# Four sums moved from POOL to DVE, and SP's flag check put ahead of its waits for the stores

## The reference

```
layer 0: graph attention: softmax over neighbours of leaky(s1_i + s2_j), times h W0
layer 1: attention by relation: scores h_i . (a_r * h_j) for adj == r, leaky, softmax, times h
layer 2: sum over relations r of (adj == r) @ h @ W_r, plus a bias
layer 3: graph attention as layer 0, with W3; its output goes through elu:
         x = x + elu(attention @ (h W3))
```

## Time and profile before

| | |
|---|---|
| three runs, median | 287.89 us |
| the profiled execution | 288.05 us, of which the span is 285.8 |
| PE busy | 274.3 us (96%) |
| ACT, DVE | 255.0 (89%), 251.9 (88%) |
| POOL | 234.1 (82%) |
| granted TensorE clock | 0.997 |

### The profile page before, as it was taken

One profiled execution on the slowest core, in us unless ns is written; L12 is line 12 of the kernel. 1 busy time (PEld: TensorE's weight loads), 2 busy tenths in 40 slices (PEclk: granted clock), 3 DMA queues, 4 the chain that ended last, 5 costly groups with the idle time before them and its releaser, 6 DMA issues.

```text
span 285.8 us, 8113 instructions
## 1 busy us (share of the span) xinstructions
PE 274.3 (96%) x2252; PEld 257.9 (90%) x2252; DVE 251.9 (88%) x1217; ACT 255.0 (89%) x850; POOL 234.1 (82%) x376
## 2 busy tenths in 40 slices
PE   3999999999999999999999999999999999998991
PEld 2999998888889999999999999888889999998991
DVE  4889999988878887899999999998898888799985
ACT  5998988799998888999999999799999889796994
POOL 4998787777747999999999988887755899999722
PEclk9999999999999999999999999999999999999998
DMA  6946645400000000015333201000000000001213
GB/s 216 319 127 179 177 142 147 167 2 2 0 0 3 0 2 2 3 37 150 98 109 114 73 22 41 18 18 2 1 2 1 3 0 0 3 3 54 76 58 115
DMA packets 15414, 17.79 MB, mean 62 GB/s; under 512 B 2180, under 2 KB 11272, under 8 KB 15368
## 3 DMA queue, kind: packets, MB, share of 16 engines
q1 hardware_dynamic: 15220, 17.18, 19.9%
q10 hardware_dynamic: 148, 0.07, 0.1%
HBM read 13.05 MB, written 4.19 MB: 60 GB/s over the span
## 4 chain that ended last, share of the span: by engine, by line
PE 87%; DVE 8%; ACT 2%; issue 1%; POOL 0%; DVEq 0%; POOLq 0%
PE bank L1001 26%; PE bank L943 10%; PE bank L919 9%; PE bank L948 9%; PE bank L877 7%; PE bank L986 5%; PE bank L956 5%; PE bank L968 5%; PE bank L998 4%; PE bank L903 3%; PE bank L950 2%; DVE pT L699 2%; DVE expy L735 1%; PE bank L922 1%; DVE st L624 1%
## 5 line engine op out<-in xcount | busy, mean ns | idle before, releaser
L367 POOL TENSOR_TENSOR rs<-mv,minus_half 128x2 f32<-128x2 f32 x128 | 89.8, 702 | 35.5 <-DVE mv L635 35.0
L1001 PE MATMUL bank<-val,pT 128*128 128x129 f32 x512 | 74.6, 275 | 0.0
L1001 PEld LDWEIGHTS bank<-val,pT 128*128 128x128 f32 x512 | 67.3, 192 | 0.0
L384 POOL TENSOR_TENSOR h<-h,rs 128x256 f32<-128x256 f32 x93 | 58.2, 626 | 2.3
L699 DVE SCALAR_TENSOR_TENSOR pT<-bank,val,edgesT 128x256 f32<-128x256 f32 x128 | 55.0, 471 | 0.8 <-PE bank L956 0.7
L624 DVE BATCH_NORM_STATS2 st<-x 128x6 f32<-128x128 f32 x192 | 45.2, 276 | 0.0
L527 ACT ACTIVATE val<-bank,val 128x128 f32<-128x128 f32 x128 | 44.3, 437 | 0.1
L635 DVE BATCH_NORM_AGGREGATE mv<-st 128x2 f32<-128x9 f32 x256 | 33.5, 172 | 10.8 <-DVE st L624 1.0
L919 PE MATMUL bank<-w_gat,hT 128*128 128x131 f32 x256 | 40.3, 281 | 0.0
L376 POOL TENSOR_TENSOR h<-x,mv 128x256 f32<-128x256 f32 x64 | 40.1, 626 | 0.0
L877 PE MATMUL bank<-ident,h 128*128 128x128 f32 x192 | 38.0, 280 | 1.4 <-ACT hT L495 1.1
(11 more groups left out here) (87 smaller groups left out, 662.7 us busy)
## 6 DMA issues: line engine op xcount, KB each, us to landing
edges<-in_adj SPq DMA_DIRECT2D x32, 256.0 KB, 2.9
xin<-in_x SPq DMA_DIRECT2D x32, 128.0 KB, 2.6
out_x<-result SPq DMA_DIRECT2D x32, 128.0 KB, 1.7
w_rel<-in_L_gnn_weight SPq DMA_DIRECT2D x1, 256.0 KB, 2.8
w_gat<-in_L_gnn_W ACTq DMA_DIRECT2D x1, 64.0 KB
w_gat<-in_L_gnn_W SPq DMA_DIRECT2D x1, 64.0 KB
a_rel<-in_L_gnn_a SPq DMA_DIRECT2D x4, 0.5 KB, 3.0
bias<-in_L_gnn_bias SPq DMA_DIRECT2D x1, 64.0 KB, 3.3
```

What stands on the lines that cost most here:

```text
L367: pool.tensor_tensor(rs[:, n % WIDE], mv[:, n % WIDE, :, 1], minus_half[:, :], ALU.pow).then_inc(rs_ready, 1)
L384: pool.tensor_tensor(h[:, n % HS, :, 0:D], h[:, n % HS, :, 0:D], rs[:, n % WIDE, :].rearrange("p (t o) -> p t o", o=1).to_broadcast([P, T, ...
L1001: last = pe.matmul(bank_o(n)[:, t], pT[:, n % 4, u, t * P:(t + 1) * P], values[:, u], start=(u == 0 and layer == 1), stop=(u == T - 1), sk ...
```

## The change

POOL_SUMS lists the graphs whose sum is made by POOL: every second one among the first sixteen, every fourth among the second sixteen (16, 20, 24, 28). DVE_SUMS are the others. `summed(g)` gives the semaphore (0 for POOL, 1 for DVE) and the count that say that the sum of g is there; the waits of SP, ACT and DVE use it. On SP, the waits for the stores go behind the load of the flag and the branch, and into the general path's start.

```diff
+POOL_SUMS = [g for g in range(B) if g % (2 if g < 16 else 4) == 0]
+DVE_SUMS = [g for g in range(B) if g not in POOL_SUMS]
...
+def summed(g):
+
+    return (0, POOL_SUMS.index(g) + 1) if g in POOL_SUMS else (1, DVE_SUMS.index(g) + 1)
...
-        result_ready = [sem("result_ready_even"), sem("result_ready_odd")]
+        result_ready = [sem("summed_by_pool"), sem("summed_by_dve")]
...
-                sp.wait_ge(result_ready[g % 2], (nth(LAST, n) + 1) // 2)
+                sp.wait_ge(result_ready[summed(g)[0]], summed(g)[1])
...
-            for k in range(SLOTS):
-                sp.wait_ge(stored[k], 16 * ROUNDS)
+            def all_stored():
+                for k in range(SLOTS):
+                    sp.wait_ge(stored[k], 16 * ROUNDS)
 
             sp.wait_ge(flag_ready, 1)
             with sp.If(sp.value_load(flag[0:1, 0:1], min_val=0, max_val=P) > 0):
+                all_stored()
                 sp.sem_inc(g_step, 1)
...
                 sp.wait_ge(g_stored, 16 * B + 16)
+            all_stored()
...
-            def add_x_even(n, layer, g):
+            def add_x_pool(n, layer, g):
                 k = g % SLOTS
-                if g % 2 == 0:
+                if g in POOL_SUMS:
...
-            pipeline([(add_x_even, 13, LAST), (add_bias, 3, RGCN_REL), (scale_deviation, 3, LAST),
+            pipeline([(add_x_pool, 13, LAST), (add_bias, 3, RGCN_REL), (scale_deviation, 3, LAST),
...
-                    act.wait_ge(result_ready[g % 2], (nth(LAST, n) - 3) // 2)
+                    act.wait_ge(result_ready[summed(g - 4)[0]], summed(g - 4)[1])
...
-                    dve.wait_ge(result_ready[g % 2], (g - WIDE) // 2 + 1)
+                    dve.wait_ge(result_ready[summed(g - WIDE)[0]], summed(g - WIDE)[1])
...
-                if g % 2 == 1:
+                if g in DVE_SUMS:
```

## The result

The changed kernel takes 290.17 us (median of four, 289.72 to 290.29) against 287.89: 0.75% slower, ratio 1.0075 with a 95% interval of 1.0061 to 1.0088. Forecast were 287.9 us and a range of 287.0 to 289.0. The sign is that of rival B; the place of the loss is partly another one.

The account below looks back on a forecast made before the run. DVE sets the order until 263.6 us, PE is full from 265.7 to 276.3, then the pipeline drains. SP -0.5, the end +0.15 and PE +0.35 sum to 0.0 us: 287.9 us, range 287.0 to 289.0.

Parts of the forecast that it names:

- rival B: Slower, chance 0.14: POOL, moved forward, blocks DVE's two-input operations between 261.6 and 265.6 us; 289.7 or 289.0 us.
- step 3: Sum of 18 on DVE makes rinv of graph 22 0.34 us later; less 0.14 slack, PE loses 0.20 us.
- Step 4: POOL's h operations, 0.7 us earlier, meet one of three DVE operations in part: 0.15 us, bounds 0 and 1.4.
- Step 2: Four sums of 0.72 us leave POOL; its h come up to 0.7 us earlier; relief counted as 0.
- Steps 5 and 6: DVE's late sums: 22 falls in idle time, 26 loses 0.05 us, 30 makes the last sum 0.15 us late.
- step 6: Sum of 30 before DVE's last sum: +0.34 us, less 0.18 from the last elu; taken as 0.15 us late.
- Step 7: SP's flag load and branch ahead of its store waits: the end comes 0.5 us earlier, bounds 0 and 1.0.
- Rival E: Same, chance 0.10: SP gains nothing, since the last stores land later or the engines' end waits elsewhere; 288.4 us.
- Rival D: Faster, chance 0.12: the long elu at 256.89 us does not come back; it cost PE 1.08 us; 286.8 us.

Follow-up runs that it names:

- e6: Kernel before, with only the sums of graphs 22, 26 and 30 moved from POOL to DVE, SP as before: 288.15 us, ratio 0.9998.
- e7: Kernel before, with the sum of graph 18 left out altogether, other even sums on POOL, SP as before: 288.94 us, ratio 1.0024.
- e3: Kernel before, with only the sum of graph 18 moved from POOL to DVE, SP as before: 289.14 us, ratio 1.0043.
- e11: Kernel before, with only the sum of graph 16 moved from POOL to DVE, SP as before: 288.51 us, ratio 1.0021.
- e8: Kernel before, with PE leaving out its flag wait, load, branch and general loop: 287.70 us, ratio 0.9980.
- e10: Kernel before, with SP's edit alone and PE without flag wait, load, branch and general loop: 287.05 us, ratio 0.9968.
- e9: Changed kernel, with PE leaving out its flag wait, load, branch and general loop: 288.53 us, ratio 1.0013.

## Why the prediction was wrong

**The reading of who bounds what (right).** The loss sits where DVE leads PE, the three late sums cost nothing (e6), and the sum of 18 makes rinv late by its 0.3 us with ACT and PE behind it, as step 3 had it. Step 3's slack was sized too large. It counted from the end of hT at 267.77. But at the two gaps of the earlier trace rows the transpose began 0.15 and 0.14 us behind the end of hT, and 0.06 and 0.05 us behind the end of the read of the accumulator that belongs to it. Here that read ends at 267.85:

```profile
267.61 0.24 ACT L495 ACTIVATION_READ_ACCUMULATOR hT<-bank 128x1 f32 x1
```

That leaves 0.12 us less the 0.05 of the signal, about 0.07 and not 0.14, and a loss of 0.27 and not 0.20; between e7 and e3 PE's last group moves by 0.32.

**Step 4, collisions (failed; a term mis-sized).** I expected one of three DVE operations to meet POOL in part and put 0.15 us; two met it and waited 0.45 and 0.59 us. With them the value of steps 3 and 4 together is 1.36 us at PE and not 0.35. The bound of 1.4 us held, but I did not carry it into the range. The mechanism was named, in the step and in rival B, whose sign, an operation over 0.8 us, came twice (0.89 and 1.00). What I had in hand and did not use is the order of the starts: POOL's scaling would start at 261.57, the subtraction 0.57 later, at 262.14, and DVE's sum of 17 stood at 262.14; a hand retiming of three POOL operations says that they meet. It does not say how long DVE waits: in the kernel before, the same sum met POOL's sum of 18, begun 0.57 us earlier, and took 0.44.

The Trainium skill (SBUF — State Buffer, Who interferes with whom) has the second one blocked until the first is done. The sum of 17 waited for one subtraction, 0.45 us, but that subtraction is recorded as beginning 0.01 us after it; by the rule it would have had to issue first, and starts so close do not tell. The elu of 19 (two operations) and the long elu (three, and two in e11) go beyond the rule: in these cases DVE stayed out through every large POOL operation that followed without a pause, until the small rs operation or, for the elu of 19, until POOL stood idle.

**Step 2, the relief counted as nothing (failed in sign).** POOL's h come earlier and nobody uses it, as I said; but moving them is the loss itself. e7 isolates it at 0.8 us of idle PE, 1.04 us by distance and 0.7 to 0.8 us of time. I valued a change on an engine off the path by what it frees and not by where it puts that engine's next operations.

**Steps 5 and 6 (right in what happens, step 6 a little too high).** No loss at the sums of 22 and 26; the last elu is at 0.42 us; in e6 the flag's last operation comes at 283.45 against 283.44, where step 6 had it 0.15 us later.

**Step 7, SP (right in the span, failed in the time).** The span behind the flag fell by 0.4 us, against 0.5 forecast. The step failed where the sum took the 2.2 us around the span as fixed. They are not: SP's edit alone gives its 0.4 us back there, and in the changed kernel 1.1 us is added. I treated the last instruction of the span as the end of the program; e8 to e10 show that the end depends on PE's way out, which no row of the span shows as late. Rival E had it ("the engines' end waits elsewhere"), at a chance of 0.10.

**Rival D** is refuted for the traces: the elu of 17 takes 2.34 to 2.36 us in every one that keeps POOL's order ahead of it. For this elu, what looked like chance is the program. One execution without a trace stands apart: e9 once took 286.59 us with a span of 284.8, 1.9 us under its median of twelve, and whether it had the waits is not known.

The account: in the profiled executions the flag's last operation is 1.40 us later against the long elu, the changed one was 0.44 us ahead at that elu, and the span behind the flag is 0.4 us shorter. That makes 0.56 us of span (measured 286.4 - 285.8 = 0.6); with 1.07 us more around it, it is the difference of 289.72 - 288.05 = 1.67. Without the chance lead of 0.44 us it is 1.40 - 0.4 + 1.1 = 2.1 us, against 2.28 between the medians.

None of the full kernels beats the one before. e8 and e10 do, by 0.2% and 0.3%, without the general path of PE, so they are a bound on what the end still holds, and not a replacement.

## What to carry to other kernels

Before work is taken off an engine whose operations keep those of a busier one waiting, as POOL's do DVE's here, retime its next two or three operations against the other's operations with two SBUF inputs: taking one addition of 0.72 us away cost 0.7 to 0.8 us here. A saving behind the last engine's last wait is worth nothing until it is known that this engine ends the program; compare the time outside of the span before and after, in several executions. And where an operation may meet a run of the other engine's, put the wait for the whole run into the range.

## What the hardware did that I had not expected

- A DVE operation with two SBUF inputs waited through one, two or three POOL operations in a row (0.45, 0.59 and 1.95 us over its 0.41 to 0.44), and got in when POOL came to an operation on 128x2 elements or stood idle. Others, begun 0.24 to 0.59 us into a POOL operation (the elus at 163.03 and 142.94 of the kernel before), got in behind that one although a large one followed, and that one then took about 0.8 to 0.9 us. What decides between the two is not settled; how far the POOL operation had come does not, by these starts.
- The waits repeat from trace to trace: the sum of 17 took 0.89 to 0.90 us in all eight traces with POOL early there, the elu of 19 took 1.00 to 1.01 in seven of these.
- The time around the span is not fixed. It took steps of about 0.25 us from 2.0 to 2.75, then 3.2 to 3.4, and 1.74 to 1.90 us without PE's branch and general path.
